# The last three tiles of a gated mixture kernel in an order written out by hand, on each engine

## The chip, the cores and the metric

The kernel runs on one core of a Trainium2 chip. The core has five engines with a queue each: TensorE (PE in the profile, with PEld for its weight loads), VectorE (DVE), ScalarE (ACT), GpSimd (POOL) and SyncE (SP). Each engine works through its own instructions in order; between engines, and between an instruction and an earlier result of its own engine, order is kept by semaphores. The metric is the device time of the core in microseconds, lower is better.

## The reference, cut to what matters

Rows `x` of 4 x 512 tokens with 512 numbers each go through two stages, both behind a layer norm and a gate:

```
x = x + tanh(g_xattn[0]) * xattn(layernorm(x), tokens, ctx, ctx, ctx)
x = x + tanh(g_ffn[0]) * ffn(layernorm(x), Wr, br, Wd, bd, Wu, bu)

def xattn(h, token_ids, Wg, Wu, Wd):     # 4 experts, picked by the token's number; here Wg = Wu = Wd
    y = (silu(h @ Wg[e].T) * (h @ Wu[e].T)) @ Wd[e]
def ffn(x, Wr, br, Wd, bd, Wu, bu):      # 8 experts of rank 16, the best two
    gates = softmax(x @ Wr + br + bonus)
    w = the two largest gates of a row, divided by their sum, else 0
    h = relu(x @ Wd[e] + bd[e])
    out = sum over e of w[e] * (h @ Wu[e] + bu[e])
```

## The kernel before

The rows are sorted by expert into T = 16 tiles of 128 rows. Since a tile can hold rows of several experts, NP = T + 3 = 19 pairs of a tile and an expert are worked through. For a pair, ACT normalizes the rows (`h`), PE turns them (`ps_hT`), and the expert's two products run (`ps_a`, then `ps_y`), each as three 16-bit products of high and low parts: ACT copies the high part out of PSUM, DVE subtracts it to get the low part. DVE adds the result to the rows (`add_y`, line 1082) and takes the sums for the second norm (`statistics2`, line 1090).

The second stage of a tile runs three steps (`LATE`) and more behind its pair: POOL gets the reciprocal root (`rstd`, line 454), ACT normalizes (`h2`, line 796), PE turns (`ps_h2T`, line 685), ACT and DVE make high and low parts (lines 815 and 1110), PE forms `ps_hid` (lines 632 to 634, "hidden product"), DVE adds the bias (`hid`, line 1124) and finds the two largest (`top8`, `gap`, `arg8`, lines 1142 to 1146). ACT takes the tanh of half the gap (line 801), POOL turns the indices into masks (`choice`, line 488), DVE blends them to the weights `w8`, the weighted rows (line 1172) and three copies of `w8` (`w_rep`, line 1176). PE turns these (`ps_wT`, lines 697 and 698), ACT and DVE make high and low parts again (lines 790 and 791; 1150 and 1151, "low parts of wtT"), PE forms the output product `ps_o` (lines 642 to 645), DVE adds it (`add_low_rank`, line 1113) and POOL scatters the tile to its rows in HBM (line 529).

Each engine's part of one step is the function `step`. `pipeline` (line 313) calls it for all steps: what a step does for each pair and tile it looks up by offsets, and equal steps go into a loop. The order in a step is thus written by hand once. The steps 19 to 22, in which no pair is begun, are drained by the same functions, with a few branches of their own (`ending` and `draining` on DVE, `has_y and not has_a` on PE). `choice` and `rstd` on POOL run in one loop over all steps (line 510). Tile numbers of a pair are read into registers (`place`, line 1077) before the add.

## Time and profile before

| | us |
|---|---|
| Median of 3 runs (lowest to highest) | 200.31 (199.83 to 200.53) |
| The profiled execution | 200.81 |
| Its span, from first to last instruction | 198.7 |
| PE busy | 173.7 (87%) |
| DVE busy | 155.5 (78%) |
| ACT busy | 105.9 (53%) |
| POOL busy | 99.5 (50%) |

A row of the profile gives an instruction by its line in the kernel, engine, operation and tiles (out<-in); times are counted from the start of the span. An instruction can begin before the one ahead of it on its engine has ended, so starts tell more of the order than busy time does. A name with a q at its end (DVEq) is the engine's sequencer, which handles registers and waits ahead of the engine itself. Tiles that end in a number lose it (`h2` stands as `h`, `w8` as `w`).

### The profile page before, as it was taken

What the parts mean: (1) busy time and instruction counts of PE and PEld (TensorE: products, weight loads), DVE (VectorE), ACT (ScalarE), POOL (GpSimd) and SP (SyncE); (2) the same over time, 40 slices, a digit from 0 to 9 for tenths busy, and PEclk for the clock granted to TensorE, in tenths of its full rate; (3) what the DMA queues carried; (4) which work ended last, traced back from release to release, by engine and by line L of the source; (5) the groups of instructions that cost most, each with busy time, mean ns of one, the idle gap of its engine ahead of it and who ended that gap; (6) DMA issues with size and microseconds to landing.
All of it is one profiled execution on the core that took longest, in us unless ns stands there. A gap on an engine that the chain in (4) does not pass through costs nothing.

```text
span 198.7 us, 4382 instructions
## 1 busy us (share of the span) xinstructions
PE 173.7 (87%) x1074; PEld 105.5 (53%) x1075; DVE 155.5 (78%) x523; ACT 105.9 (53%) x224; POOL 99.5 (50%) x246
## 2 busy tenths in 40 slices
PE   1666896999998999999999999999999999987550
PEld 1654473665554555756567565665655666553310
DVE  4859695797669799898988899877887778877840
ACT  3596599984576365363635646256462653415300
POOL 4477855508444475465735538336062351626551
PEclk9999999999999999999999999999999999999995
DMA  4937682000301201103011010110110101001121
GB/s 144 383 136 243 209 214 80 30 26 2 107 4 49 56 0 53 58 2 106 3 53 54 0 53 0 53 54 0 53 53 2 53 2 53 35 21 53 53 101 57
DMA packets 6784, 13.43 MB, mean 68 GB/s; under 512 B 2392, under 2 KB 2520, under 8 KB 6768
## 3 DMA queue, kind: packets, MB, share of 16 engines
q0 software_dynamic: 2560, 8.39, 12.6%
q1 hardware_dynamic: 4208, 4.86, 7.3%
q8 instruction: 6, 0.10, 0.2%
q14 instruction: 10, 0.08, 0.1%
HBM read 9.06 MB, written 4.19 MB: 67 GB/s over the span
## 4 chain that ended last, share of the span: by engine, by line
PE 66%; issue 7%; DMA 7%; DVE 7%; POOL 7%; SPq 1%; ACT 1%; POOLq 1%; DVEq 1%
PE ps_y L603 8%; PE ps_y L605 8%; PE ps_y L604 8%; PE ps_a L603 7%; PE ps_a L604 7%; PE ps_a L605 7%; PE ps_pT L624 4%; DMA xs<-in_x_dram,rows_of 4%; PE ps_h2T L685 3%; PE ps_hT L677 3%; DMA bu_nat<-in_L_ffn_bu_dram 3%; POOL hot_slot L432 2%; POOL xs L439 2%; PE ps_hid L632 2%; PE ps_hid L634 1%
## 5 line engine op out<-in xcount | busy, mean ns | idle before, releaser
L456 POOL TENSOR_SCALAR ve<-mv 128x1 f32<-128x1 f32 x32 | 7.6, 238 | 60.6 <-DVE mv L1099 50.1
L603 PE MATMUL ps_y<-w_hi,pT_hi 128*128 x76 | 28.8, 379 | 2.6 <-DVE w_lo L952 1.8
L783 ACT ACTIVATE pT_hi<-ps_pT 128x512 f16<-128x512 f32 x19 | 11.3, 595 | 36.0 <-PE ps_pT L624 36.0
L603 PE MATMUL ps_a<-w_hi,hT_hi 128*128 x76 | 29.6, 389 | 0.7 <-DVE hT_lo L1074 0.6
L604 PE MATMUL ps_a<-w_lo,hT_hi 128*128 x76 | 29.5, 388 | 0.0
L605 PE MATMUL ps_a<-w_hi,hT_lo 128*128 x76 | 29.3, 386 | 0.0
L604 PE MATMUL ps_y<-w_lo,pT_hi 128*128 x76 | 28.8, 379 | 0.0
L605 PE MATMUL ps_y<-w_hi,pT_lo 128*128 x76 | 28.8, 379 | 0.0
L796 ACT ACTIVATE h<-xs,mrs,rs 128x512 f32<-128x512 f32 (+1 forms) x16 | 13.0, 814 | 21.6 <-POOL mrs L458 21.6
L1086 DVE SCALAR_TENSOR_TENSOR xs<-ps_y,y_t,xs 128x512 f32 x19 | 14.3, 751 | 12.2 <-PE ps_y L605 11.5
L457 POOL TENSOR_TENSOR rs<-ve,neg_half 128x1 f32<-128x1 f32 x32 | 18.8, 587 | 2.7
L529 POOL DMA_INDIRECT out_dram<-xs,rows_of x16 | 17.3, 1082 | 5.0 <-DVE xs L1117 2.5
L824 ACT ACTIVATE h<-xs,mrs,rs 128x512 f32 (+1 forms) x19 | 15.6, 818 | 6.9 <-POOL mrs L458 4.3
L439 POOL DMA_INDIRECT xs<-in_x_dram,rows_of x16 | 17.0, 1063 | 3.7 <-issue 2.9
L805 ACT ACTIVATE silu<-ps_a,inv_bits 128x512 f32<-128x512 f32 x19 | 12.8, 675 | 4.3 <-PE ps_a L605 4.2
L1068 DVE SCALAR_TENSOR_TENSOR prod<-ps_a,prod_bits,silu 128x512 f32<-128x512 f32 x19 | 14.0, 739 | 1.1 <-ACT silu L805 1.1
L1104 DVE TENSOR_TENSOR pT_lo<-ps_pT,pT_hi 128x512 f16<-128x512 f32 x19 | 13.1, 689 | 0.7 <-ACT pT_hi L783 0.3
L1074 DVE TENSOR_TENSOR hT_lo<-ps_hT,hT_hi 128x512 f16<-128x512 f32 x19 | 12.9, 681 | 0.5 <-ACT hT_hi L810 0.3
L1117 DVE SCALAR_TENSOR_TENSOR xs<-ps_o,out_coef,xs 128x512 f32<-128x512 f32 (+1 forms) x16 | 11.9, 741 | 1.3 <-PE ps_o L645 1.2
L603 PEld LDWEIGHTS ps_y<-w_hi,pT_hi 128*128 128x128 f16 x76 | 7.6, 100 | 9.7 <-issue 3.0
L740 ACT ACTIVATE sq_act<-w_nat 128x512 f32<-128x512 f32 x16 | 10.1, 632 | 4.9 <-DMA w_nat<-in_ctx_dram 4.5
L605 PEld LDWEIGHTS ps_a<-w_hi,hT_lo 128*128 128x128 f16 x76 | 7.6, 100 | 9.2 <-issue 0.8
(209 smaller groups left out, 432.6 us busy)
## 6 DMA issues: line engine op xcount, KB each, us to landing
w_nat<-in_ctx_dram SPq DMA_DIRECT2D x4, 1024.0 KB, 7.5
xs<-in_x_dram,rows_of POOLq DMA_INDIRECT x16, 3.5
wd_nat<-in_L_ffn_Wd_dram SPq DMA_DIRECT2D x1, 256.0 KB
wu_nat<-in_L_ffn_Wu_dram SPq DMA_DIRECT2D x1, 256.0 KB
out_dram<-xs,rows_of POOLq DMA_INDIRECT x16, 2.9
b_in<-in_L_ffn_bd_dram SPq DMA_DIRECT2D x1, 64.0 KB
bu_nat<-in_L_ffn_bu_dram SPq DMA_DIRECT2D x3, 16.0 KB
tok_i<-in_itok_BxS_dram SPq DMA_DIRECT2D x1, 8.0 KB, 1.6
```

Source lines behind the costliest of these rows:

```text
L439: g.indirect_dma_start(out=xs[:, t, :], out_offset=None, in_=x_rows[:, :], in_offset=bass.IndirectOffsetOnAxis(ap=rows_of[:, t:t + 1], axi ...
L457: then(g.tensor_tensor(rs[:, n, k:k + 1], ve[:, n, k:k + 1], neg_half[:, :], ALU.pow))
L529: g.indirect_dma_start(out=out_rows[:, :], out_offset=bass.IndirectOffsetOnAxis(ap=rows_of[:, k:k + 1], axis=0), in_=x1[:, k, :], in_offse ...
L603: mm(ps[:, :], lhs_hi[:, kc, :], hi, start=(kc == 0), stop=False)
L604: mm(ps[:, :], lhs_hi[:, kc, :], lo, start=False, stop=False)
L605: last = mm(ps[:, :], lhs_lo[:, kc, :], hi, start=False, stop=(kc == KC - 1))
L796: a(h2[:, :], flat(x1[:, col(k), :]), ACT.Identity, bias=mrs[:, 1, col(k)], scale=rs[:, 1, col(k)]).then_inc(normed2, 1)
L824: a(h[:, :], flat(xs[:, col(tile), :]), ACT.Identity, bias=mrs[:, 0, col(tile)], scale=rs[:, 0, col(tile)]).then_inc(normed1, 1)
L1068: v.scalar_tensor_tensor(prod[:, :], ps_a[:, :], prod_t[:, col(k)], silu[:, :], ALU.mult, ALU.mult).then_inc(prod_done, 1)
L1074: v.tensor_tensor(hT_lo[:, :, :], ps_hT[:, :, :], hT_hi[:, :, :], ALU.subtract).then_inc(hT_lo_done, 1)
L1086: v.scalar_tensor_tensor(flat(x1[:, col(tile), :]), ps_y[:, :], y_t[:, col(k)], flat(xs[:, col(source), :]), ALU.mult, ALU.add).then_inc(x ...
L1104: v.tensor_tensor(pT_lo[:, :, :], ps_pT[:, :, :], pT_hi[:, :, :], ALU.subtract).then_inc(pT_lo_done, 1)
```

## The change

All steps up to 18 stay as they are; `pipeline` stops there. For the rest every engine gets a function `drain` that lists its instructions one by one for the tiles 12 to 15.

- The second norm of tiles 14 and 15: DVE adds the epsilon (`variance`), POOL takes the power only, and DVE normalizes (`norm2`), where POOL did three instructions and ACT the normalization.
- The masks of tiles 13 to 15: DVE makes them (`choose`) instead of POOL.
- The copies of `w8` for tiles 13 to 15 are made by ACT (`repeat_w`) instead of DVE.
- The output product of tiles 12 and 13 is taken out of PSUM by ACT (`take_out`) and added by POOL (`add_taken`) instead of by DVE.
- Tile 15 is turned into two PSUM banks (`ps_hT`, `ps_pT`), two quarters in each, and its high and low parts are made by halves.
- The order of the rest is new. On PE the hidden product of tile 13 stands ahead of the transposes of the last expert product.

```diff
+                if first == NP:
+                    break
+                last = min(last, NP)
...
+            def scatter(k, done=None):
+
+                pool.wait_ge(*(done or (out_done, k + 1)))
+                g.indirect_dma_start(
+                    out=out_rows[:, :],
+                    out_offset=bass.IndirectOffsetOnAxis(ap=rows_of[:, k:k + 1], axis=0),
+                    in_=x1[:, k, :], in_offset=None,
+                ).then_inc(s_scatter, 16)
+
+            def power(n, k):
+
+                pool.wait_ge(var_done, n)
+                g.tensor_tensor(rs[:, 1, k:k + 1], ve[:, 1, k:k + 1], neg_half[:, :],
+                                ALU.pow).then_inc(rstd2, 1)
+
+            def add_taken(n, k):
+
+                pool.wait_ge(o_taken, n)
+                g.tensor_tensor(x1[:, k, :], taken[:, n - 1, :], x1[:, k, :],
+                                ALU.add).then_inc(added, 1)
+
+            for i in range(-3, NP):
...
-                if 0 <= k < T:
+                if 0 <= k < T - 2:
                     pool.wait_ge(aggr2, k + 1)
                     rstd(1, mv2, k, rstd2)
+
+            scatter(T - 5)
+            power(1, T - 2)
+            power(2, T - 1)
+            add_taken(1, T - 4)
+            scatter(T - 4, (added, 1))
+            add_taken(2, T - 3)
+            scatter(T - 3, (added, 2))
+            scatter(T - 2, (out_done, T - 3))
+            scatter(T - 1, (out_done, T - 2))
...
+            def drain():
+
+                last = NP - 1
+                e_last = expert_of(last)
+                hidden_product(T - 3)
+                transpose_product(last)
+                second_product(last, e_last)
+                transpose_h2(T - 2)
+                low_rank_out(T - 4)
+                hidden_product(T - 2)
+
+                pe.wait_ge(normed2, T)
+                for c in range(KC):
+                    half = tr((ps_hT, ps_pT)[c // 2][:, c % 2, :], h2[:, c:D:KC], ident[:, :])
+                    if c % 2:
+                        half.then_inc(h2T_last, 1)
+                pe.wait_ge(w_rep_done, 1)
+                transpose_weighted(T - 3)
+
+                pe.wait_ge(hid_done, T - 1)
+                for c in range(KC):
+                    pe.wait_ge(lo_last, c // 2 + 1)
+                    mm(ps_hid[:, 0:HC], hT_hi[:, c, :], w_in_hi[:, c, :], start=(c == 0), stop=False)
+                    mm(ps_hid[:, 0:HC], hT_hi[:, c, :], w_in_lo[:, c, :], start=False, stop=False)
+                    done = mm(ps_hid[:, 0:HC], hT_lo[:, c, :], w_in_hi[:, c, :],
+                              start=False, stop=(c == KC - 1))
+                done.then_inc(hid_mm, 1)
+                low_rank_out(T - 3, (o_taken, 1))
+                pe.wait_ge(w_rep_done, 2)
+                transpose_weighted(T - 2)
+                low_rank_out(T - 2, (o_taken, 2))
+                pe.wait_ge(w_rep_done, 3)
+                transpose_weighted(T - 1)
+                low_rank_out(T - 1, (out_done, T - 3))
+
...
+            def repeat_w(n, k):
+
+                act.wait_ge(w8_done, k + 1)
+                act.wait_ge(wtT_done, k)
+                a(w_rep[:, :, 0:EF], w8[:, :].unsqueeze(1).to_broadcast([P, 3, EF]), ACT.Copy,
+                  scale=s_ffn[:, 0:1]).then_inc(w_rep_done, 1)
+
+            def take_out(n, k):
+
+                act.wait_ge(o_mm, k + 1)
+                a(taken[:, n - 1, :], ps_o[:, :], ACT.Copy, scale=out_coef[:, :]).then_inc(o_taken, 1)
+
+            def drain():
+
+                pT_high(NP - 1)
+                wtT_high(T - 4)
+                tanh_of_gap(T - 3)
+                h2T_high(T - 2)
+                take_out(1, T - 4)
+                repeat_w(1, T - 3)
+                for n, bank in enumerate((ps_hT, ps_pT)):
+                    act.wait_ge(h2T_last, n + 1)
+                    a(hT_hi[:, 2 * n:2 * n + 2, :], bank[:, 0:2, :], ACT.Copy).then_inc(hi_last, 1)
+                wtT_high(T - 3)
+                tanh_of_gap(T - 2)
+                repeat_w(2, T - 2)
+                take_out(2, T - 3)
+                wtT_high(T - 2)
+                tanh_of_gap(T - 1)
+                repeat_w(3, T - 1)
+                wtT_high(T - 1)
+
...
+            def variance(n, k):
+
+                dve.wait_ge(aggr2, k + 1)
+                v.tensor_scalar(ve[:, 1, k:k + 1], mv2[:, 1:2], EPS, None, ALU.add).then_inc(var_done, 1)
+
+            def norm2(k):
+
+                dve.wait_ge(rstd2, k + 1)
+                dve.wait_ge(h2T_done, k)
+                v.tensor_scalar(h2[:, :], x1[:, k, :], mv2[:, 0:1], rs[:, 1, k:k + 1],
+                                ALU.subtract, ALU.mult).then_inc(normed2, 1)
+
+            mixed = [0]
+
+            def then_mix(ins):
+
+                mixed[0] += 1
+                ins.then_inc(mix_step, 1)
+                dve.wait_ge(mix_step, mixed[0])
+
+            def choose(n, k):
+
+                dve.wait_ge(arg_done, k + 1)
+                then_mix(v.tensor_copy(arg8f[:, :], arg8[:, :]))
+                v.tensor_scalar(half_first[:, :], slot_no[:, 0:EF], arg8f[:, 0:1], 0.5,
+                                ALU.is_equal, ALU.mult)
+                then_mix(v.tensor_scalar(half_second[:, :], slot_no[:, 0:EF], arg8f[:, 1:2], 0.5,
+                                         ALU.is_equal, ALU.mult))
+                v.tensor_tensor(half_sum[:, :], half_first[:, :], half_second[:, :], ALU.add)
+                v.tensor_tensor(half_dif[:, :], half_first[:, :], half_second[:, :],
+                                ALU.subtract).then_inc(mixed_last, 1)
+                dve.wait_ge(mixed_last, n)
+                dve.wait_ge(tanh_done, k + 1)
+
+            def drain():
+
+                pT_low(NP - 1)
+                statistics2(T - 2)
+                variance(1, T - 2)
+                hidden(T - 3)
+                top_two(T - 3)
+                choose(1, T - 3)
+                wtT_low(T - 4)
+                norm2(T - 2)
+                add_y(NP - 1, *place(NP - 1))
+                statistics2(T - 1)
+                variance(2, T - 1)
+                h2T_low(T - 2)
+                norm2(T - 1)
+                dve.wait_ge(wtT_done, T - 3)
+                blend(T - 3).then_inc(weighted_done, 1)
+                hidden(T - 2)
+                top_two(T - 2)
+                for n, bank in enumerate((ps_hT, ps_pT)):
+                    dve.wait_ge(hi_last, n + 1)
+                    v.tensor_tensor(hT_lo[:, 2 * n:2 * n + 2, :], bank[:, 0:2, :],
+                                    hT_hi[:, 2 * n:2 * n + 2, :], ALU.subtract).then_inc(lo_last, 1)
+                wtT_low(T - 3)
+                choose(2, T - 2)
+                dve.wait_ge(wtT_done, T - 2)
+                dve.wait_ge(w_rep_done, 1)
+                blend(T - 2).then_inc(weighted_done, 1)
+                hidden(T - 1)
+                top_two(T - 1)
+                wtT_low(T - 2)
+                choose(3, T - 1)
+                dve.wait_ge(wtT_done, T - 1)
+                dve.wait_ge(w_rep_done, 2)
+                blend(T - 1).then_inc(weighted_done, 1)
+                add_low_rank(T - 2)
+                wtT_low(T - 1)
+                add_low_rank(T - 1)
```

PE around the end of step 18, before (hidden product of tile 13: `ps_hid`; transposes of the last product: `ps_pT`):

```order
L697 MATMUL ps_wT<-ident,weighted 128x128 [waits wtT_lo_done,weighted_done]
L698 MATMUL ps_wT<-ident,w_rep 96x128
L610 TENSOR_LOAD expert_i
L610 ISA x2
L624 MATMUL ps_pT<-ident,prod 128x128 [waits prod_done]
L624 MATMUL ps_pT<-ident,prod 128x128 x3
L632 MATMUL ps_hid<-w_in_hi,h2T_hi 128x136 [waits hid_done,h2T_lo_done]
L633 MATMUL ps_hid<-w_in_lo,h2T_hi 128x136
L634 MATMUL ps_hid<-w_in_hi,h2T_lo 128x136
```

and now:

```order
L700 MATMUL ps_wT<-ident,weighted 128x128 [waits wtT_lo_done,weighted_done]
L701 MATMUL ps_wT<-ident,w_rep 96x128
L649 TENSOR_LOAD expert_i
L649 ISA x2
L671 MATMUL ps_hid<-w_in_hi,h2T_hi 128x136 [waits hid_done,h2T_lo_done]
L672 MATMUL ps_hid<-w_in_lo,h2T_hi 128x136
L673 MATMUL ps_hid<-w_in_hi,h2T_lo 128x136
...
L673 MATMUL ps_hid<-w_in_hi,h2T_lo 128x136
L663 MATMUL ps_pT<-ident,prod 128x128 [waits prod_done]
L663 MATMUL ps_pT<-ident,prod 128x128 x3
L642 ISA [waits x1_done,pT_lo_done]
L642 MATMUL ps_y<-w_hi,pT_hi 128x512
```

The 12 matmuls of the hidden product now stand ahead of the four transposes, and with these all that waits for `pT_lo_done`.

DVE from the search for the indices of tile 13 to the registers of the last add of `ps_y`, before:

```order
L1146 MAX_INDEX arg8<-top8,hid 128x8
L1150 TENSOR_TENSOR wtT_lo<-ps_wT,wtT_hi 128x128 [waits wtT_hi_done]
L1151 TENSOR_TENSOR gwT<-ps_wT,gwT 8x128
L1079 TENSOR_LOAD pair_tile_i
L1079 ISA x2
L1080 TENSOR_LOAD source_i
L1080 ISA x2
L1086 ISA [waits x1_done,y_done]
L1086 REGISTER_ALU
L1086 SCALAR_TENSOR_TENSOR xs<-ps_y,y_t,xs 128x512
```

and now:

```order
L1255 MAX_INDEX arg8<-top8,hid 128x8
L1336 CAST arg8f<-arg8 128x8 [waits arg_done]
L1337 TENSOR_SCALAR half_first<-slot_no,arg8f 128x8 [waits mix_step]
L1339 TENSOR_SCALAR half_second<-slot_no,arg8f 128x8
L1341 TENSOR_TENSOR half_sum<-half_first,half_second 128x8 [waits mix_step]
L1342 TENSOR_TENSOR half_dif<-half_first,half_second 128x8
L1260 TENSOR_TENSOR wtT_lo<-ps_wT,wtT_hi 128x128 [waits wtT_hi_done,tanh_done,mixed_last]
L1261 TENSOR_TENSOR gwT<-ps_wT,gwT 8x128
L1322 TENSOR_SCALAR h2<-xs,mv2,rs 128x512 [waits h2T_done,rstd2]
L1200 TENSOR_LOAD pair_tile_i
L1200 ISA x2
L1201 TENSOR_LOAD source_i
```

Five instructions of the masks have come in between, and the low parts of wtT (`wtT_lo`, first row of two) wait for the last of them (`mixed_last`) and for the tanh; the normalization of tile 14 (`h2`) follows, and the register loads come behind them.

POOL in the drain, before (scatter of tile 11, norm of tile 15, first instruction of the choice of tile 14):

```order
L529 DMA out_0_dram<-xs,rows_of 2048x512 [waits out_done]
L456 TENSOR_SCALAR ve<-mv2 128x1 [waits aggr2]
L457 TENSOR_TENSOR rs<-ve,neg_half 128x1 [waits rs_step]
L458 TENSOR_SCALAR mrs<-mv2,rs 128x1 [waits rs_step]
L491 CAST arg8f<-arg8 128x8 [waits arg_done]
```

and now, from the scatter of tiles 10 and 11 to the last:

```order
L526 DMA out_0_dram<-xs,rows_of 2048x512 [waits out_done] x2
L535 TENSOR_TENSOR rs<-ve,neg_half 128x1 [waits var_done] x2
L541 TENSOR_TENSOR xs<-taken,xs 128x512 [waits o_taken]
L526 DMA out_0_dram<-xs,rows_of 2048x512 [waits added]
L541 TENSOR_TENSOR xs<-taken,xs 128x512 [waits o_taken]
L526 DMA out_0_dram<-xs,rows_of 2048x512 [waits added]
L526 DMA out_0_dram<-xs,rows_of 2048x512 [waits out_done] x2
```

The power of tile 15 (the second of the two `rs`) is followed at once by the add of tile 12, which waits for ACT's copy alone.

## Rows read from the trace of the kernel before

**Rows 1.** Stretches: us, busy of each engine (instructions), granted clock, DMA share, GB/s.
```profile
175.00:185.00 10.00, 7.34 (x52) 4.19 (x50) 7.93 (x32) 4.29 (x11) 4.75 (x14) 1.00 0.07 28
185.00:195.00 10.00, 4.85 (x28) 2.01 (x28) 6.01 (x20) 1.33 (x6) 5.78 (x13) 0.90 0.20 79
```

**Rows 2.** PE in order of time: start us, us, line, operation, out<-in.
```profile
175.02 0.22 PE L632 MATMUL ps_hid<-w_in_hi,h2T_hi 128*128 128x136 f16 x1
...
175.67 0.22 PE L634 MATMUL ps_hid<-w_in_hi,h2T_lo 128*128 128x136 f16 x1
```

**Rows 3.** DVE in order of time from 175 us.
```profile
175.85 0.69 DVE L1104 TENSOR_TENSOR pT_lo<-ps_pT,pT_hi 128x512 f16<-128x512 f32 x1 [0.29 <-ACT pT_hi L783]
...
177.20 0.18 DVE L1099 BATCH_NORM_AGGREGATE mv<-st 128x2 f32<-128x6 f32 x1
...
177.29 0.28 DVE L1124 TENSOR_TENSOR hid<-ps_hid,b_s 128x136 f32<-128x136 f32 x1
...
178.00 0.15 DVE L1146 FIND_INDEX8 arg<-top,hid 128x8 uint32<-128x8 f32 x1
...
179.71 0.75 DVE L1086 SCALAR_TENSOR_TENSOR xs<-ps_y,y_t,xs 128x512 f32 x1 [1.08 <-PE ps_y L605]
...
181.24 0.18 DVE L1099 BATCH_NORM_AGGREGATE mv<-st 128x2 f32<-128x6 f32 x1
```

**Rows 4.** DVE's sequencer, 176 to 181 us: durations ns, first to last start.
```profile
L1079 DVEq TENSOR_LOAD <-pair_tile_i x1: 304/304/304, 177.8 to 177.8; - x1
...
L1080 DVEq SEQ_ASSERT  x1: 23/23/23, 179.0 to 179.0; - x1
...
L1086 DVEq FUSED_REGOPS  x1: 105/105/105, 179.5 to 179.5; - x1
```

**Rows 5.** DVE in order of time at 22 us, each waiting for the one before.
```profile
22.30 0.15 DVE L987 CAST half_exp_f<-half_exp 128x2 f32<-128x2 int32 x1
22.48 0.36 DVE L989 TENSOR_SCALAR exp_of<-expert_f,half_exp_f 128x2 f32<-128x2 f32 x2
22.87 0.16 DVE L992 TENSOR_REDUCE exp_t<-exp_of 128x2 f32<-128x4 f32 x1
```

**Rows 6.** POOL in order of time: variance and power of tile 15.
```profile
181.52 0.24 POOL L456 TENSOR_SCALAR ve<-mv 128x1 f32<-128x1 f32 x1 [0.16 <-DVE mv L1099]
181.84 0.57 POOL L457 TENSOR_TENSOR rs<-ve,neg_half 128x1 f32<-128x1 f32 x1
```

**Rows 7.** The last tile in order of time, ACT and DVE.
```profile
182.92 0.81 ACT L796 ACTIVATE h<-xs,mrs,rs 128x512 f32<-128x512 f32 x1
...
185.19 0.69 DVE L1110 TENSOR_TENSOR h2T_lo<-ps_h2T,h2T_hi 128x512 f16<-128x512 f32 x1 [0.23 <-ACT h2T_hi L815]
...
187.08 0.74 DVE L1117 SCALAR_TENSOR_TENSOR xs<-ps_o,out_coef,xs 128x512 f32<-128x512 f32 x1
...
187.75 0.16 DVE L1142 MAX8 top<-hid 128x8 f32<-128x8 f32 x1
...
190.07 0.29 DVE L1172 SCALAR_TENSOR_TENSOR weighted<-hid,w 128x128 f32<-128x128 f32 x1
...
191.51 0.29 DVE L1150 TENSOR_TENSOR wtT_lo<-ps_wT,wtT_hi 128x128 f16<-128x128 f32 x1 [0.22 <-ACT gwT L791]
...
193.34 0.75 DVE L1117 SCALAR_TENSOR_TENSOR xs<-ps_o,out_coef,xs 128x512 f32<-128x512 f32 x1 [1.24 <-PE ps_o L645]
```

**Rows 8.** Groups by line and shape: count, busy us, mean ns, idle before.
```profile
L506 POOL TENSOR_TENSOR w_lo<-w_full,w_hi 128x512 f16<-128x512 f32 x2 | 2.3, 1155 | 7.4 <-ACT w_hi L752 7.4
...
L1029 DVE TENSOR_SCALAR b_s<-b_in,ffn_bits 128x136 f32<-128x136 f32 x1 | 0.3, 258 | 0.0
```

**Rows 9.** POOL beside DVE at 7.7 us, in order of time.
```profile
7.71 1.77 POOL L432 TENSOR_SCALAR hot_slot<-slot_no,in_tile_f 128x128 f16<-128x128 f32 x1 [4.68 <-DVE in_tile_f L916]
...
7.86 1.22 DVE L919 TENSOR_TENSOR hot_slot<-in_tile_f,slot_no 128x1024 f16<-128x1024 f16 x1
```

**Rows 10.** POOL's line 432: count, ns min/median/max, first and last start.
```profile
L432 POOL TENSOR_SCALAR hot_slot<-slot_no,in_tile_f x4: 600/788/1767, 7.7 to 11.0; 128x128 f16<-128x128 f32 x4
```

174 lines of the change are left out of this document (86 added, 88 removed).

## The prediction

> **What bounds the kernel now.** I read the page first, then busy time by stretches, then instructions in order of time over the last 25 us, since the change touches nothing before that. On the page PE is busy 87% of a span of 198.7 us, and its tenths stand at 9 until slice 35, from about 174 us on at 8, 7, 5, 5, 0. The reader is to see in the stretches [rows 1] that DVE outlasts PE there: from 175 to 185 us it is busy 7.93 of 10 us beside PE's 7.34, from 185 to 195 us 6.01 beside 4.85. So the drain (the steps after the last pair has begun) hangs on a chain that runs through DVE again and again, and what an engine idles matters less than when DVE comes to an instruction. The granted clock is 1.00 to 185 us and 0.90 after it; the page's last slice has it at half, its lower level.
>
> Everything below is a walk along DVE's instructions, step against step, with tile 15 (the last) as the one that ends the kernel. The difference in the time at which its last add starts is the forecast, because what follows that add (one scatter, its transfer, the end) is the same in both kernels.
>
> **Step 1, PE: hidden product before the transposes.** Before, PE turns the last product first and then runs the hidden product of tile 13; the change swaps them. The hidden product is 12 matmuls; the first starts at 175.02 and the twelfth at 175.67 [rows 2], 0.059 each, 0.71 in all. The transposes, ACT's copy, DVE's subtraction (start 175.85 [rows 3]) and the last expert product each come 0.71 later. Nothing hides it: DVE waits for the subtraction, and the hidden product was lying in that wait before.
>
> **Step 2, DVE: variance and choice of tile 13.** The variance waits for the aggregate's result. Before, the next instruction (hid, 177.29) was issued 0.09 after the aggregate (177.20) [rows 3]; now the aggregate's 0.18, 0.03 for the wait and some 0.08 to issue lie between: +0.20. So the index search, 178.00 before [rows 3], stands at 178.91. Then come the five instructions of the choice, which POOL did beside. Their waits are priced from three DVE instructions early in the kernel that wait for each other just so [rows 5]: a cast to the next instruction 0.18, a pair of masks to the next 0.39. With 0.19 from the search to the cast and 0.28 for sum and difference (an estimate: 0.16 and 0.03 as in those rows, and the other instruction's issue) that is 1.04: release at 179.95. The bounds: 0.65, if half the waits go under; 1.35, with POOL's slower durations.
>
> **Step 3, DVE: the registers of the last y-add.** Before, DVE's sequencer ran ahead: the first register load stands at 177.8, before the search at 178.00 had even started, and the last check at 179.0 [rows 4]; 1.22 us, hidden behind the expert product. In the change the instruction in front of those loads that waits is the low part of wtT, which waits for the choice's last result. So they begin at 179.98 and end at 181.20. From the operation on registers at 179.5 [rows 4] to the add at 179.71 [rows 3] is 0.2; with the release 0.25. The add starts at 181.45, against 179.71: +1.74. The expert product (0.71 late) is ready well before. The low parts of wtT for tile 12 and the normalization of tile 14 run under these loads and cost nothing; if the loads could still run ahead (0.6 instead of 1.22, the lower bound), they'd be what stands there, and 0.6 comes back.
>
> **Step 4, the norm of tile 15.** From add to aggregate start is 1.53 [rows 3], its length 0.18; variance 0.19; handing to POOL 0.10 (181.42 to 181.52), the power 0.57 [rows 6], and 0.09 back: the normalization starts at 184.11. Before, ACT's started at 182.92 [rows 7], so +1.19: a gain of 0.55 within the step. ACT took 0.81 for it [rows 7]. No row has DVE's 128x512 scalar operation from SBUF; the same operation with 136 elements takes 0.258 [rows 8], with 2 elements 0.22 (0.36 for two, of which the second starts 0.14 later [rows 5]), so 0.36 at 512 by that slope; upper bound 0.74, the 128x512 add with a scalar (187.08 [rows 7]). I take 0.36, the row of the same operation: end at 184.47 against 183.73, +0.74. At 0.74 the whole would come 0.4 later.
>
> **Step 5, turning tile 15 into two banks.** PE is free for it at 184.72, and ACT's two half copies are ready at about 185.5 and 185.8 (0.38 each, an estimate from the page's 0.595 for the whole). DVE gets there no sooner: normalization, blend of tile 13, hid and search of tile 14 hold it to 185.78 (0.29, 0.6 and 0.78, the last from 177.29 to 178.00 [rows 3] and one issue). Two half subtractions end at 186.51; before, the whole one ended at 185.88 [rows 7]: +0.63. The halves bring nothing that DVE could use.
>
> **Step 6, the queue after it.** DVE now does the low parts of wtT for tile 13 (0.59: two instructions of 0.29 [rows 7]), choice and blend of tile 14 (0.9 and 0.6), and only then hid of tile 15, at 188.5, although PE has had it since 187.1. The maximum follows at 188.84. Before it stood at 187.75, held there by the add of 187.08 [rows 7], which is now taken over by ACT and POOL: +1.09 (without that help +1.7). Low parts of tile 14, wait for ACT's copy, choice of tile 15: its weighted rows start at 191.23, against 190.07: +1.16. The repeat of w8 on ACT lies beside weighted and saves 0.15; the half clock that stretched the last matmuls before (0.1) is already in the row. Last add at 194.2 against 193.34 [rows 7]: **+0.86**.
>
> POOL's two adds of 128x512 take some 1.15 each (its subtraction of that shape, [rows 8]) and end, scatters included, by 191.5, before the scatter of tile 14 can go: nothing on the path. ACT's two copies of the output product: idle time of ACT, 5.6 of the 20 us busy.
>
> Against its own profiled execution (200.81, span 198.7 and 2.1 around it) the sum gives 201.7. That execution lay 0.5 above the median of the runs, 200.31; on the median the sum gives **201.2**. A measurement of this kernel tells about 0.3% (0.6 us) from no change.
>
> **A wait of DVE on POOL (rival B).** In this trace a POOL instruction that reads SBUF beside a DVE instruction with two SBUF inputs is the one that waits: POOL's mask at 7.71 took 1.77 while DVE's 1.22 ran from 7.86 [rows 9], where its shortest took 0.60 [rows 10]; DVE's 1024 elements kept their 1.2. In the change, POOL's first add starts the moment its power for tile 15 ends (184.02), 0.09 before DVE's normalization of tile 15, and lasts 1.15. If DVE waits for it, the normalization starts at 185.15 and every later step moves by 1.0: +1.9, 202.2. For it: the add comes first, and nothing of DVE in this trace is of this kind and size. Against it: in rows 9 DVE wasn't held.
>
> The Trainium skill, SBUF — State Buffer, section "Who interferes with whom", states that DVE's scalar operation from SBUF to SBUF can take both port pairs, and that then whichever of DVE and POOL starts first has the shared pair for its whole instruction. By that rule the normalization is held, as in rival B; the trace agrees for POOL's side alone (1.77 in place of 0.60), and no run here shows DVE's.
>
> **Rival C, the clock.** PE will idle more between 175.3 and 177.4 and after 180 us. The clock fell once before, in the last 6 us. If it falls by 185 us, the hidden products (0.71 each), the turns and the output products run at the lower level; on the path that is some 0.3 for tile 15's hidden product and 0.75 for its output product (3 times 0.21 more): +1.6 to +2, 202.1. For it: more idle; against it: with PE busy only 4.85 of 10 us the clock still stood at 0.90 over 185 to 195 us [rows 1].
>
> **Rival D, faster: DVE's queue doesn't bind.** Then only tile 15's own chain counts: norm by POOL 0.55 shorter, normalization 0.45, half copies 0.5, the add of 187.08 no longer ahead of the maximum 0.65, choice 0.6, w8 0.15: -2.9, and +0.9 for steps 1 and 2: -2.0, 198.3; with half of it 199.3. It decides from the point where the last y-add starts within 0.3 of the expert product, 180.4 instead of 181.45. For it: each of these gains is real on its own. Against it: DVE was busy 79% of 175 to 185 us already [rows 1], and the change adds three choices (some 2.7), two normalizations (0.6) and two variances (0.4) and removes two adds (1.3) and three repeats (0.5).
>
> **Rival E, no change:** loads still ahead (-0.6) and choices at their lower bound; 200.3.
>
> **How the numbers follow.** Forecast (0.5 to 1.4 more) 0.45; B 0.20; C 0.08; D 0.17; E 0.10. Forecast, B and C lie over +0.6 with 0.31, 0.19, 0.08: slower 0.58. Within 0.6: 0.14, 0.09 from E and 0.02 of D: 0.25. Faster: 0.17 (0.15 of D, 0.02 of the others). The range reaches from the middle of D and E, 199.6, to B and C, 202.4; the forecast's own is 200.8 to 201.7.
>
> **What would show it.** Right: the last y-add 1.5 us or more after the end of DVE's last choice mask, DVE hardly idle from 184 to 192 us, the last maximum some 2 us after its PE product. B: the last normalization takes 1.4 or begins after POOL's add ends. Wrong: y-add within 0.3 of the expert product, the transposes not 0.7 later, or a choice under 0.6.

## The result and the profile after

The changed kernel takes 203.95 us (median of 4 runs, 203.21 to 205.87), against 200.07 for the kernel before on the same chip: ratio 1.0213, 95% interval [1.0128, 1.0299]. The forecast was 201.2, its range ended at 202.4. Slower was right; the size was not. The profiled execution took 203.24, its span is 201.5. Now and then one execution of a kernel takes 1.5% or more above the fastest of that kernel; such ones are left out of all medians and ratios here.

First the stretches of the changed kernel, in the columns of [rows 1]:

```profile
175.00:185.00 10.00, 6.02 (x42) 3.26 (x39) 7.98 (x29) 2.50 (x6) 2.55 (x4) 1.00 0.08 28
185.00:195.00 10.00, 5.80 (x31) 3.55 (x32) 8.55 (x38) 3.96 (x14) 4.17 (x5) 0.83 0.14 53
```

VectorE (DVE) has as much to do as before in the first ten microseconds and 2.5 us more in the second ten (8.55 against 6.01), although two of its adds went to other engines. To set the steps against those of before, both traces need a common point: the y-add of pair 17, the last instruction ahead of the drain. In the trace before, and then in the changed kernel's with the instructions that answer to [rows 3] and [rows 7]:

```profile
174.81 0.75 DVE L1086 SCALAR_TENSOR_TENSOR xs<-ps_y,y_t,xs 128x512 f32 x1 [0.48 <-PE ps_y L605]
```

```profile
174.66 0.75 DVE L1207 SCALAR_TENSOR_TENSOR xs<-ps_y,y_t,xs 128x512 f32 x1 [0.48 <-PE ps_y L644]
...
176.43 0.69 DVE L1225 TENSOR_TENSOR pT_lo<-ps_pT,pT_hi 128x512 f16<-128x512 f32 x1 [1.01 <-ACT pT_hi L848]
...
178.76 0.16 DVE L1255 FIND_INDEX8 arg<-top,hid 128x8 uint32<-128x8 f32 x1
178.95 0.17 DVE L1336 CAST arg8f<-arg 128x8 f32<-128x8 uint32 x1
...
179.84 0.29 DVE L1260 TENSOR_TENSOR wtT_lo<-ps_wT,wtT_hi 128x128 f16<-128x128 f32 x1
...
180.46 0.55 DVE L1322 TENSOR_SCALAR h<-xs,mv,rs 128x512 f32<-128x512 f32 x1
181.49 0.75 DVE L1207 SCALAR_TENSOR_TENSOR xs<-ps_y,y_t,xs 128x512 f32 x1 [0.48 <-issue]
...
184.04 1.48 DVE L1322 TENSOR_SCALAR h<-xs,mv,rs 128x512 f32<-128x512 f32 x1
...
186.91 0.40 DVE L1368 TENSOR_TENSOR hT_lo<-ps_hT,hT_hi 128x256 f16<-128x256 f32 x1
...
190.15 0.17 DVE L1251 MAX8 top<-hid 128x8 f32<-128x8 f32 x1
...
190.95 0.29 DVE L1260 TENSOR_TENSOR wtT_lo<-ps_wT,wtT_hi 128x128 f16<-128x128 f32 x1 [0.30 <-ACT gwT L855]
...
191.57 0.40 DVE L1336 CAST arg8f<-arg 128x8 f32<-128x8 uint32 x1
...
193.00 0.29 DVE L1269 SCALAR_TENSOR_TENSOR weighted<-hid,w 128x128 f32<-128x128 f32 x1
...
196.16 0.75 DVE L1238 SCALAR_TENSOR_TENSOR xs<-ps_o,out_coef,xs 128x512 f32<-128x512 f32 x1 [1.27 <-PE ps_o L687]
```

Ahead of the last y-add (181.49), VectorE's sequencer (DVEq) loads its two registers (durations in ns, first to last start):

```profile
L1200 DVEq TENSOR_LOAD <-pair_tile_i x1: 314/314/314, 179.9 to 179.9; - x1
...
L1201 DVEq SEQ_ASSERT  x1: 23/23/23, 181.1 to 181.1; - x1
```

The line to look at is 184.04: the same instruction that took 0.55 for tile 14 (180.46) takes 1.48 for tile 15. The cast, 0.17 for tile 13, takes 0.40 for tile 15 (191.57). Neither row shows a wait before its start: the instruction begins and then lasts longer. GpSimd (POOL) in the same trace, its power and its two adds:

```profile
183.45 0.55 POOL L535 TENSOR_TENSOR rs<-ve,neg_half 128x1 f32<-128x1 f32 x1 [4.66 <-DVE ve L1316]
183.97 1.27 POOL L541 TENSOR_TENSOR xs<-taken,xs 128x512 f32<-128x512 f32 x1
...
190.69 1.25 POOL L541 TENSOR_TENSOR xs<-taken,xs 128x512 f32<-128x512 f32 x1 [4.13 <-ACT taken L878]
```

The normalization lies beside the first add (183.97 to 185.24), the cast beside the second (190.69 to 191.94), and they end 0.28 and 0.03 us after it. ScalarE (ACT) ahead of the low parts of tile 14 (190.95):

```profile
189.91 0.69 ACT L878 ACTIVATE taken<-ps_o,out_coef 128x512 f32<-128x512 f32 x1 [0.19 <-PE ps_o L687]
190.49 0.27 ACT L854 ACTIVATE wtT_hi<-ps_wT 128x128 f16<-128x128 f32 x1
```

Last, TensorE (PE) and its clock: the stretches of five microseconds, and two successive hidden products of tile 15.

```profile
185.00:190.00 5.00, 4.09 (x24) 3.00 (x24) 4.50 (x21) 2.11 (x8) 1.27 (x2) 0.66 0.14 52
190.00:195.00 5.00, 1.71 (x9) 0.54 (x8) 4.05 (x18) 1.85 (x7) 2.89 (x3) 1.00 0.14 54
```

```profile
187.53 0.32 PE L727 MATMUL ps_hid<-w_in_lo,hT_hi 128*128 128x136 f16 x1
187.64 0.32 PE L728 MATMUL ps_hid<-w_in_hi,hT_lo 128*128 128x136 f16 x1
```

They start 0.11 apart where those of [rows 2] stood 0.06 apart: the granted clock was at its lower level (1.2 GHz) there, 0.66 as a mean over 185 to 190 us, and back at 1.00 after it.

### The profile page after: what moved, and what is told of

Read it like the earlier page. It is cut to its first block, busy times and chain, and to the rows that moved or that the text cites. A ratio compares the mean times of both kernels' runs of the same rounds, so it can differ in the third digit from the quotient of the medians.

```text
span 201.5 us, 4385 instructions
## 1 busy us (share of the span) xinstructions
PE 172.6 (86%) x1074; PEld 105.3 (52%) x1075; DVE 159.1 (79%) x538; ACT 106.4 (53%) x228; POOL 97.1 (48%) x229
## 4 chain that ended last, share of the span: by engine, by line
PE 65%; DVE 10%; DMA 7%; issue 6%; POOL 5%; SPq 1%; DVEq 1%; ACT 1%; POOLq 1%
PE ps_y L642 7%; PE ps_y L644 7%; PE ps_y L643 7%; PE ps_a L642 7%; PE ps_a L643 6%; PE ps_a L644 6%; DMA xs<-in_x_dram,rows_of 4%; PE ps_pT L663 4%; PE ps_h2T L693 3%; PE ps_hT L767 3%; DMA bu_nat<-in_L_ffn_bu_dram 2%; POOL hot_slot L445 2%; PE ps_hid L671 2%; POOL xs L452 2%; PE ps_hid L673 2%
## 5 line engine op out<-in xcount | busy, mean ns | idle before, releaser
L469 POOL TENSOR_SCALAR ve<-mv 128x1 f32<-128x1 f32 x30 | 7.1, 238 | 56.5 <-DVE mv L1220 45.2
L642 PE MATMUL ps_a<-w_hi,hT_hi 128*128 x76 | 28.8, 379 | 0.7 <-DVE hT_lo L1195 0.6
L643 PE MATMUL ps_a<-w_lo,hT_hi 128*128 x76 | 28.8, 379 | 0.0
L644 PE MATMUL ps_a<-w_hi,hT_lo 128*128 x76 | 28.8, 379 | 0.0
L921 ACT ACTIVATE h<-xs,mrs,rs 128x512 f32<-128x512 f32 (+1 forms) x14 | 11.4, 815 | 18.9 <-POOL mrs L471 18.9
L470 POOL TENSOR_TENSOR rs<-ve,neg_half 128x1 f32<-128x1 f32 x30 | 17.7, 588 | 2.5
L671 PE MATMUL ps_hid<-w_in_hi,h2T_hi 128*128 128x136 f16 x60 | 11.3, 223 | 1.6 <-DVE h2T_lo L1231 1.6
L767 PE MATMUL ps_hT<-ident,h 128*128 128x128 f32 x76 | 12.0, 281 | 0.6 <-ACT h L944 0.6
```

Source lines behind the costliest of these rows:

```text
L470: then(g.tensor_tensor(rs[:, n, k:k + 1], ve[:, n, k:k + 1], neg_half[:, :], ALU.pow))
L642: mm(ps[:, :], lhs_hi[:, kc, :], hi, start=(kc == 0), stop=False)
L643: mm(ps[:, :], lhs_hi[:, kc, :], lo, start=False, stop=False)
L644: last = mm(ps[:, :], lhs_lo[:, kc, :], hi, start=False, stop=(kc == KC - 1))
L671: mm(ps_hid[:, 0:HC], h2T_hi[:, c, :], w_in_hi[:, c, :], start=(c == 0), stop=False)
L767: last = tr(ps_hT[:, c, :], h[:, c * P:(c + 1) * P], ident[:, :])
```

## The experiments

Fourteen kernels ran, in four sets, on the chips numbered 7 (a0, e1, e4, e5), 3 (c1 to c4), 11 (d1 to d4) and 15 (g1, g2), each with the kernel before beside it. The medians of the kernel before there are 201.26, 201.05, 201.06 and 201.01, so between sets compare the column "over", the median less the kernel before's of the same set. The last three columns come from each one's profiled execution, in microseconds after the y-add of pair 17: the last y-add, the weighted rows of tile 15, the last add.

| Kernel | median us (runs) | over | ratio to before [95%] | last y-add | weighted 15 | last add |
|---|---|---|---|---|---|---|
| before, first chip | 200.07 (4) | | | 4.90 | 15.26 | 18.53 |
| changed, first chip | 203.95 (4) | 3.88 | 1.0213 [1.0128, 1.0299] | 6.83 | 18.34 | 21.50 |
| a0: changed again | 203.56 (6) | 2.30 | 1.0154 [1.0093, 1.0214] | 6.82 | 18.65 | 21.68 |
| e1: first add later | 203.59 (5) | 2.33 | 1.0100 [1.0066, 1.0133] | 6.81 | 19.18 | 23.32 |
| e4: e1, loads, turn first | 202.90 (7) | 1.64 | 1.0092 [1.0060, 1.0124] | 5.87 | 17.03 | 21.17 |
| e5: 16 idle products | 203.79 (7) | 2.53 | 1.0129 [1.0098, 1.0160] | 6.82 | 17.94 | 21.82 |
| c1: both adds clear | 202.50 (11) | 1.45 | 1.0072 [1.0046, 1.0099] | 6.82 | 16.77 | 20.91 |
| c2: adds on VectorE | 203.89 (5) | 2.84 | 1.0137 [1.0103, 1.0172] | 6.82 | 18.33 | 22.21 |
| d4: c1, loads | 201.59 (8) | 0.53 | 1.0031 [1.0004, 1.0058] | 6.36 | 16.29 | 20.17 |
| c3: c1, loads, turn first | 201.15 (12) | 0.10 | 1.0003 [0.9980, 1.0027] | 5.87 | 15.82 | 19.95 |
| c4: c2, loads, turn first | 202.71 (6) | 1.66 | 1.0099 [1.0060, 1.0137] | 5.86 | 17.32 | 21.20 |
| d1: c3, idle products at the end | 200.69 (12) | -0.37 | 1.0000 [0.9970, 1.0029] | 5.86 | 15.85 | 18.88 |
| d2: c3, choice of 13 on GpSimd | 200.27 (12) | -0.79 | 0.9963 [0.9941, 0.9985] | 5.12 | 15.08 | 19.21 |
| d3: d1 and d2 | 199.76 (11) | -1.30 | 0.9956 [0.9923, 0.9989] | 5.12 | 15.07 | 18.11 |
| g1: changed, 28 idle products | 202.79 (11) | 1.78 | 1.0061 [1.0024, 1.0099] | 6.82 | 17.96 | 20.99 |
| g2: c1, 13 idle products | 201.74 (11) | 0.73 | 1.0041 [1.0006, 1.0076] | 6.82 | 17.54 | 20.57 |

**a0, the changed kernel again.** No edit.

> The changed kernel once more, beside the three edits of it that follow. Both theories: some 3 to 4 us over the kernel before, with DVE's normalization of tile 15 at about 1.5 us and a lower clock somewhere between 185 and 190 us. Open is why its runs spread from 203.2 to 205.9 while those of before lay within 1.3 us.

Measured 203.56, 2.30 over the kernel before, less than the 3 to 4 expected; normalization 1.48, cast 0.40 as on the first chip. Both holds thus came in both traces.

**e1, the first add later.** GpSimd's first add waits until VectorE's normalization of tile 15 has ended:

```diff
+            pool.wait_ge(normed2, T)
             add_taken(1, T - 4)
```

> POOL's first add waits until the normalization of tile 15 has ended. Theory hold (POOL's add of 128x512, begun 0.07 us earlier, holds DVE's normalization for its whole length): the normalization takes 0.55 instead of 1.48 us and the last add starts about 0.9 us earlier, so the time falls by 0.7 to 1.2 us. Rival clock (the excess over the forecast is TensorE's lower clock from 185 to 189 us): the normalization may shorten, but the time falls by less than 0.3 us.

The normalization went back to 0.55, and yet the median stayed, 2.33 over the kernel before, as the rival had it. (The ratio fell, from 1.0154 to 1.0100, but the intervals overlap. The profiled execution took 205.41, so of it only durations are read.) VectorE and then GpSimd in e1:

```profile
184.34 0.55 DVE L1323 TENSOR_SCALAR h<-xs,mv,rs 128x512 f32<-128x512 f32 x1
184.80 0.22 DVE L1267 SCALAR_TENSOR_TENSOR w<-half_dif,half_tanh,half_sum 128x8 f32<-128x8 f32 x1
185.06 1.33 DVE L1270 SCALAR_TENSOR_TENSOR weighted<-hid,w 128x128 f32<-128x128 f32 x1
```

```profile
184.97 1.27 POOL L541 TENSOR_TENSOR xs<-taken,xs 128x512 f32<-128x512 f32 x1 [0.66 <-DVE h L1323]
```

The add now lay beside the weighted rows, whose two inputs both come from SBUF: 1.33 in place of 0.29. The hold had not gone, it had moved by two instructions. So the kind of instruction counts that lies beside the add, not this one place. In this trace the granted clock was 0.67 over 185 to 190 us and 0.50 over 190 to 195 as well.

**e4, e1 with loads early and the transposes first.** The row address of the last y-add is loaded at the start of the drain, and PE turns the last product before the hidden product of tile 13:

```diff
+                where_last = place(NP - 1)
                 pT_low(NP - 1)
...
-                add_y(NP - 1, *place(NP - 1))
+                add_y(NP - 1, *where_last)
...
+                transpose_product(last)
                 hidden_product(T - 3)
-                transpose_product(last)
```

> Three edits at once: POOL's add waits as in the run before, DVE loads the registers of the last y-add at the start of the drain, PE turns the last product ahead of the hidden product of tile 13. Theory queue and hold: the last y-add starts about 1.3 us earlier than in the changed kernel (0.7 by the turn, 0.6 by the loads), the last add 2.2 us earlier (with 0.9 from the hold): 201 to 201.5 us where the changed kernel takes 203.3. Rival clock: all three move DVE but the end moves by less than 0.8 us, since PE's slow stretch stays.

The last y-add came 0.96 earlier, at 5.87; the weighted rows of tile 13 were held again (1.33), the clock stood at its lower level for the last output product, and 202.90 came out instead of 201 to 201.5: a miss.

**e5, idle products.** Sixteen products of 128x512 into a bank that nobody reads any more, in PE's pauses from the transposes of the last pair to those of tile 15 (`idle_products(n)` repeats one matmul n times).

> The changed kernel with 16 more products of 128x512 on PE, whose results nobody reads, laid where PE idled between 175.5 and 185.5 us (6 before the last expert product, 3 behind it, 5 and 2 around the hidden product of tile 14). Theory hold: the clock stays at 1.00 from 185 to 190 us and the last add starts 0.4 to 0.9 us earlier, no more; the normalization still takes 1.5. Rival clock: the time falls by 2 us or more and the spread of the runs falls to that of before.

The clock, then, in three stretches of e5:

```profile
185.00:190.00 5.00, 3.60 (x34) 2.27 (x33) 4.67 (x17) 1.86 (x7) 2.81 (x3) 1.00 0.13 52
190.00:195.00 5.00, 2.69 (x17) 0.98 (x14) 4.36 (x24) 1.77 (x6) 2.24 (x2) 1.00 0.01 2
195.00:199.00 4.00, 2.29 (x6) 0.58 (x6) 1.77 (x4) 0.44 (x2) 0.96 (x1) 0.66 0.34 131
```

It stayed at 1.00 where the changed kernel had 0.66, and the weighted rows of tile 15 came at 17.94 instead of 18.34. It then fell at the last output product, whose matmuls took 0.61 to 0.63, and the gain was lost; neither theory had this. The time alone would have said that the clock doesn't matter. (This execution took 205.60, and 2 us of that lie ahead of the drain: its y-add of pair 17 stands at 176.66, in the other traces at 174.1 to 175.3.)

**c1, both adds clear.** Both adds are kept, but each starts where VectorE reads PSUM and one SBUF tile:

```diff
+            pool.wait_ge(arg_done, T - 1)
             add_taken(1, T - 4)
             scatter(T - 4, (added, 1))
+            pool.wait_ge(weighted_done, T)
             add_taken(2, T - 3)
```

> The changed kernel, but GpSimd's two adds start at places where VectorE reads PSUM and one SBUF tile: the first after the index search of tile 14 (it then lies beside the half subtractions and the low parts of wtT), the second after the weighted rows of tile 15. Theory 1 (GpSimd's 128x512 add, both inputs from SBUF, holds VectorE's instructions that need both SBUF read ports, wherever it starts): the normalization of tile 15 takes 0.55 instead of 1.48, the weighted rows of tile 13 0.29 (they took 1.33 in e1), the cast of tile 15 0.17 instead of 0.40; the last add, 21.5 us after the add of pair 17 in the changed kernel, comes at 20.3 to 20.6, time 202.3 to 202.6. Rival (what counts is TensorE's lower clock or the length of VectorE's queue, and the holds are taken up by other waits, as e1 seemed to say): the three durations shrink, but the last add stays after 21.2 and the time over 203.2.

VectorE and GpSimd in c1:

```profile
184.12 0.55 DVE L1324 TENSOR_SCALAR h<-xs,mv,rs 128x512 f32<-128x512 f32 x1
...
184.83 0.29 DVE L1271 SCALAR_TENSOR_TENSOR weighted<-hid,w 128x128 f32<-128x128 f32 x1
...
186.32 0.41 DVE L1370 TENSOR_TENSOR hT_lo<-ps_pT,hT_hi 128x256 f16<-128x256 f32 x1
186.65 0.28 DVE L1262 TENSOR_TENSOR wtT_lo<-ps_wT,wtT_hi 128x128 f16<-128x128 f32 x1
...
190.36 0.17 DVE L1338 CAST arg8f<-arg 128x8 f32<-128x8 uint32 x1
```

```profile
186.16 1.26 POOL L541 TENSOR_TENSOR xs<-taken,xs 128x512 f32<-128x512 f32 x1 [2.08 <-DVE arg L1257]
...
191.90 1.25 POOL L541 TENSOR_TENSOR xs<-taken,xs 128x512 f32<-128x512 f32 x1 [3.13 <-DVE weighted L1271]
```

All three held instructions have their own length back, and the two that now lie beside the first add (186.32 and 186.65, one input from PSUM) keep theirs: 0.41 and 0.28, against 0.41 and 0.29 in the changed kernel, where no add lies beside them. The weighted rows of tile 15 come at 16.77 instead of 18.65 in a0, and the time over the kernel before is 1.45 instead of 2.30. From the weighted rows to the last add it takes 4.14, in a0 3.03: the last output product of c1 ran at the lower clock.

```profile
193.72 0.61 PE L686 MATMUL ps_o<-wu_hi,wtT_hi 128*128 128x512 f16 x1 [1.15 <-DVE gwT L1263]
194.12 0.63 PE L687 MATMUL ps_o<-wu_lo,wtT_hi 128*128 128x512 f16 x1
```

The theory had the durations and the time (202.50) right, the last add a little too early (20.91 for 20.3 to 20.6), because of that clock.

**c2 and c4, the adds back on VectorE.** VectorE adds tile 12 where it waits for GpSimd's power, tile 13 ahead of the low parts of wtT(14); ACT's copies and GpSimd's adds are gone. c4 has the loads and the order of e4 as well.

```diff
                 h2T_low(T - 2)
+                add_low_rank(T - 4)
                 norm2(T - 1)
...
                 top_two(T - 1)
+                add_low_rank(T - 3)
                 wtT_low(T - 2)
...
```

> The changed kernel, but VectorE adds tiles 12 and 13 itself, out of PSUM: tile 12 between the low part of h2T(14) and the normalization of tile 15, where it waits for GpSimd's power anyway, tile 13 before the low parts of wtT(14). ACT's two copies and GpSimd's two adds are gone. Theory 1: no VectorE instruction is held (0.55, 0.29, 0.17 us); the first add costs 0.1 to 0.2 beyond the wait it fills, the second about 0.4; the last add at 20.7 to 21.0 after the add of pair 17, 202.7 to 203.0. Rival (taking two adds from VectorE was worth their 0.66 each, as the change intends): the last add comes at 21.9 or later, 203.9 or more.

> c2_dve_adds with the loads early and the transposes first. Theory: last y-add at 5.87, last add at 19.8 to 20.0, 201.8 to 202.0. Rival: 202.7 or more.

A miss: no hold is left, but 203.89 and 202.71, each over 1 us above its twin with the adds on GpSimd (c1 202.50, c3 201.15). The clock fell earlier than in the twin (0.90, 0.76 and 0.93 over the three stretches from 180 to 195 us in c2, 1.00, 1.00 and 0.63 in c1); no run separates its share from that of the adds. The rival's times (203.9 and 202.7 or more) came: with nothing held, the two adds on VectorE cost more than a microsecond, the clock's share included.

**d4 and c3, the steps 1 and 3 of the prediction undone.** d4 is c1 with the loads early, c3 also has PE's old order (both edits as in e4).

> c1_clear with the register loads of the last y-add at the start of the drain, and no other change: half of what lies between c1 and c3. Theory (loads, then the choice and the normalization queued before the add, decide): y-add at 6.25 to 6.4 instead of 6.82, last add at 20.3 to 20.5 instead of 20.91, time 202.0 to 202.2; the other 0.5 to 0.9 to c3 then is the order of product and transposes. Rival (the loads alone made the whole delay of step 3): y-add at 5.7, time 201.4.

> c1_clear with the register loads of the last y-add at the start of the drain and the last product turned before the hidden product of tile 13. Theory: the three parts add: last y-add at 5.87 as in e4 (6.83 in the changed kernel, 4.90 before), last add at 19.4 to 19.6, 201.4 to 201.6. Rival (some other chain, TensorE at its lower clock, takes over): last add at 20.5, 202.5, as little as e4 gained.

The y-adds came as the theories had them (6.36 and 5.87), the times a little lower than expected, c3's last add later (19.95 for 19.4 to 19.6). Over the kernel before, the loads bring 0.92 (1.45 to 0.53), the order of product and transposes another 0.43 (to 0.10); the last add moves by 0.74 and 0.22. c3 takes as long as the kernel before.

**d1, d2, d3, on from there.** d1 is c3 with 13 idle products around the turns of the last two tiles' weighted rows; d2 is c3 with the choice of tile 13 left on GpSimd, between its two powers; d3 is both.

```diff
             power(1, T - 2)
+            choice(T - 3)
             power(2, T - 1)
...
                 top_two(T - 3)
-                choose(1, T - 3)
                 wtT_low(T - 4)
...
```

> c3_clear_three with 13 idle 128x512 products on TensorE in its pauses between 187.4 and 193 us (2 and 5 around the turn of the weighted rows of tile 14, 2 and 4 around that of tile 15), each 0.22 long, into a bank that nobody reads any more. Theory (the lower clock at the end costs the four last output matmuls 0.2 each and the turn 0.15): those matmuls take 0.38 to 0.39 instead of 0.61 to 0.63, the last add comes 0.8 to 1.0 earlier (19.0 to 19.2 after the add of pair 17, from 19.95), time 200.2 to 200.5. Rival (the fall of the clock is only put off to the next piece, as in e5, or comes earlier): no gain, 201.1.

> c3_clear_three with the choice of tile 13 on GpSimd, between its two powers, as the kernel before has it. Theory (VectorE's queue decides in front of the last y-add): the y-add comes at 5.0 to 5.2 instead of 5.87, the last add at 19.1 to 19.3 instead of 19.95, time 200.3 to 200.5. Rival (GpSimd's small masks and VectorE's instructions with two SBUF inputs hold each other, or the power of tile 15 comes late): y-add at 5.1 but the blend of tile 13 late, last add after 19.7, 201.0.

> d1 and d2 together: if each does what its theory says, last add at 18.2 to 18.5, time 199.4 to 199.8, below the kernel before; else what remains of the two.

In d1 the last output product ran at the full clock, with the stretch at 1.00 where c3 had 0.61 (the stretch in c3 and in d1, then d1's output product):

```profile
190.00:195.00 5.00, 3.26 (x10) 0.79 (x7) 2.38 (x10) 0.75 (x3) 3.21 (x3) 0.61 0.13 52
190.00:195.00 5.00, 2.88 (x13) 0.94 (x11) 2.54 (x6) 0.75 (x3) 3.52 (x4) 1.00 0.15 58
```

```profile
192.16 0.39 PE L686 MATMUL ps_o<-wu_hi,wtT_hi 128*128 128x512 f16 x1 [0.29 <-DVE gwT L1272]
192.39 0.38 PE L687 MATMUL ps_o<-wu_lo,wtT_hi 128*128 128x512 f16 x1
```

The last add is 1.07 earlier than in c3's trace, the time 0.47 lower, and the ratios (1.0003 and 1.0000) don't tell the two apart. c3's profiled execution was its longest (202.00), so its clock may have cost less in the others; that is not shown. In d2 the choice on GpSimd brings the last y-add to 5.12, where it waits for the expert product again, and 0.89 of the time:

```profile
179.19 0.75 DVE L1210 SCALAR_TENSOR_TENSOR xs<-ps_y,y_t,xs 128x512 f32 x1 [0.31 <-PE ps_y L647]
```

d2 and d3 are faster than both kernels; d3 takes 199.76, ratio 0.9956 [0.9923, 0.9989], within the 199.4 to 199.8 expected.

**g1 and g2, the clock's share.** g1 is the changed kernel, holds and all, with idle products through the whole drain; g2 is c1 with 13 of them at the end, so neither holds nor, as meant, the lower clock.

> The changed kernel, holds and all, with 28 idle 128x512 products in TensorE's pauses from the last pair's transposes to the last output product (the 16 of e5 and 12 more around the turns of the weighted rows of tiles 14 and 15). Theory (of the time over the forecast, the holds of VectorE by GpSimd's adds and TensorE's lower clock are two separate parts): normalization of tile 15 still 1.4 to 1.5, cast of tile 15 still held, but every output matmul at 0.38 to 0.39; weighted rows of tile 15 at 17.9 to 18.0 as in e5, last add at 20.8 to 20.95 (21.5 to 21.7 in the changed kernel), time 202.9 to 203.1. Rival (the clock was of no consequence): last add after 21.4, 203.5.

> c1_clear with 13 idle products around the turns of the weighted rows of tiles 14 and 15: the changed kernel with neither the holds nor the lower clock, and so the case that the forecast of the prediction walked through. If the walk was right but for these two, weighted rows of tile 15 at 16.7 to 16.8 after the add of pair 17 (the walk: 16.42), last add at 19.9 to 20.05 (the walk: 19.39), time 201.9 to 202.2. Rival (a third part is missing): weighted rows or last add 0.5 later than that.

In g1 the clock stood at 1.00 throughout, while the normalization still took 1.48 and the cast 0.34:

```profile
185.00:190.00 5.00, 3.39 (x27) 1.94 (x25) 4.50 (x21) 2.02 (x8) 1.40 (x2) 1.00 0.13 52
190.00:195.00 5.00, 4.60 (x22) 1.82 (x22) 4.04 (x18) 1.67 (x7) 3.14 (x3) 1.00 0.14 54
```

Last add 20.99, time 202.79: the clock's own share in the changed kernel is 0.52 of the time (2.30 in a0 to 1.78), 0.5 to 0.7 in the traces. g2 has 201.74, ratio 1.0041. Its profile was less clean than meant, since the clock fell ahead of the idle products there:

```profile
180.00:185.00 5.00, 2.63 (x18) 1.89 (x19) 4.25 (x13) 1.58 (x3) 0.55 (x1) 0.85 0.02 3
185.00:190.00 5.00, 4.68 (x33) 3.03 (x32) 3.95 (x20) 2.33 (x9) 2.30 (x2) 0.81 0.08 30
```

```profile
185.56 0.30 DVE L1256 TENSOR_TENSOR hid<-ps_hid,b_s 128x136 f32<-128x136 f32 x1 [0.56 <-PE ps_hid L675]
```

VectorE waited 0.56 for the hidden product of tile 14 there. That put its weighted rows at 17.54, against 16.7 to 16.8 expected, and the last add at 20.57; from the one to the other it is 3.03, as at the full clock in d1. c1, with the same program up to the output product of tile 13, had its weighted rows at 16.77, with the clock at 1.00 to 190 us.

## Why the prediction was wrong

The step that failed is the overlap of GpSimd's two adds with VectorE. The prediction's sum has "nothing on the path" for them; the runs show that each held a VectorE instruction that was on it, the normalization of tile 15 for 0.93 us and the cast of tile 15 for 0.23. Beside that the normalization was mis-sized (0.36 for 0.55), and the fall of the clock, which the sum leaves out, came.

Step by step, in microseconds after the y-add of pair 17 (174.81 taken from the walk's times), with c1 as the same program without these two holds:

| | walk | changed | c1 |
|---|---|---|---|
| step 1: pT_lo starts | 1.75 | 1.77 | 1.76 |
| step 2: choice releases | 5.14 | 5.18 | 5.17 |
| step 3: last y-add | 6.64 | 6.83 | 6.82 |
| step 4: normalization of tile 15 starts | 9.30 | 9.38 | 9.38 |
| step 4: it ends | 9.66 | 10.86 | 9.93 |
| step 6: last MAX8 | 14.03 | 15.49 | 14.42 |
| step 6: weighted rows of tile 15 | 16.42 | 18.34 | 16.77 |
| last add | 19.39 | 21.50 | 20.91 |

**Steps 1 to 3** hold to 0.2 us: the swap on PE, the choice (1.04 by the walk, 1.08 from the search at 178.76 to the low part at 179.84), and register loads that can't run ahead. They stand at 179.9 to 181.1, and in the changed row of the y-add what ends its idle time is "issue", no longer PE: the sequencer is late, not the data. The edits of d4 and c3 gave both back: the y-add comes 0.46 and 0.49 earlier, where the forecast had 0.6 and 0.71 (the 0.49 lacks 0.22 that the early loads cost, see below).

**Step 4** went wrong in two ways. The length of an unhindered normalization is 0.55, not 0.36: it lies between the bounds of 0.36 and 0.74, and the end that was taken, from a row of 136 elements, was the wrong one (+0.19). And the hold by GpSimd's add, put aside as rival B with a chance of 0.20, did come: 1.48 for 0.55, +0.93, where B's sign was 1.4. c1 takes it away by a place for the add alone.

**Step 5** came out in its sense: in the changed kernel the first half subtraction starts (186.91) right behind the index search of tile 14, so VectorE was what the halves waited for.

**Step 6** had the queue right: MAX8 of tile 15 came 1.74 after the end of its product in c1, as in the walk (188.84 less 187.1). It missed the second hold. The prediction checked the one instruction that the first add meets, and said of GpSimd's adds that nothing of them lies on the path. The second add lies beside the choice of tile 15, which the change itself had put on VectorE: cast +0.23. ACT's copy of tile 13, "idle time of ACT" in the prediction, stood on the path too, since its output product came late (rival C below): the high parts of tile 14 start behind it (189.91, then 190.49), and VectorE's low parts wait 0.30 for them (190.95). With both holds gone, MAX8 and the weighted rows of c1 stand 0.39 and 0.35 behind the walk, most of which is there by the end of the normalization (0.27). From the weighted rows to the last add the walk takes 2.97, against 3.27 before, and gives a reason for 0.15 of these 0.30, or 0.25 with the half clock's 0.1; at the full clock it took 3.03 (g1, d1), so the end was about right without its sum being complete.

**Rival C**, the clock, was half true as well. It was to fall by 185 us and cost 0.3 at tile 15's hidden product and 0.75 at its output product. It fell in 185 to 190 us, over the turns and the hidden product of tile 15 and the first matmul of the next output product, and again only at the last matmul of all (0.51 for 0.38). The first fall made the output product of tile 13 late, and with it ACT's copy and VectorE's low parts of tile 14. Together it cost 0.52 by the times of a0 and g1. The reason given against it (4.85 busy of 10 us and still 0.90 before) did not carry over: with 5.80 busy the clock was 0.83.

In the changed kernel's trace the last add stands 2.11 behind the walk: 1.16 are the two holds, 0.19 the length of the normalization, 0.30 the wait for ACT, 0.13 the last matmul; 0.33 are small lags that no run separates.

So the forecast described the case without B and C, and that case is g2: ratio 1.0041 [1.0006, 1.0076], where +0.86 on 200.31 is 1.0043. The agreement is in part luck. The interval is wide, the trace was not free of the clock, and the forecast took the 2.1 us around the span to be the same in both kernels. On the chips of the experiments they are 2.09 to 2.20 in every run of the kernel before and 1.70 to 1.88 in every run of the others, so some 0.4 is gained outside the span, for a reason that no run shows; the span of g2 is 1.1 longer than before (200.0 against 198.9). What the changed kernel takes beyond g2 is the holds, 0.85 (a0 to c1) or 1.05 (g1 to g2), and the clock, 0.52 (a0 to g1) or 0.72 (c1 to g2). These shares are estimates: the intervals of the four ratios overlap, all but a0's with g2's, and the durations in the traces are the firmer evidence. (On the chips of the experiments the change costs 2.30; on the first it was 3.88, from four runs of 203.21 to 205.87 us, of which only that of 203.24 has a trace, so the other 1.6 stay open.) The two rivals were given apart, each as if the other failed; the range ended where one of them came true, and both did.

What misled was one reading of [rows 9]. There GpSimd's instruction, started 0.15 earlier, was the one that grew, and it was taken to speak against a hold of VectorE. It showed that such a pair can hold one another; which one loses it did not show for the pairs to come. Here GpSimd started 0.07 (184.04) and 0.09 us (e1) ahead and VectorE lost for as long as the add lasted.

The Trainium skill, SBUF — State Buffer, section "Who interferes with whom", names just these instructions: a scalar operation or a cast in a two-port mode, and any VectorE instruction with two SBUF inputs beside a GpSimd instruction that reads SBUF. It adds that one with at most one SBUF input and outside such a mode does not contend. The runs agree on each: 1.48 for 0.55, 0.40 for 0.17, 1.33 for 0.29, and 0.41 and 0.28 unchanged beside c1's add; in which mode an instruction ran no trace shows. That whichever starts first has the pair, as the prediction cites it, the starts in the traces bear out for GpSimd's adds, but not in [rows 9], where GpSimd started first and lost.

In c3 the first low part starts 0.22 later (1.26) than before (1.04), although PE's order is alike. The chain of c3's profile shows why: the early register loads stand in front of it and end only then.

```profile
176.16 0.02 DVEq L1203
176.19 0.05 issue
176.23 0.70 DVE pT_lo L1227
```

The same 0.22 is all that is left of the y-add's delay in d2 (5.12 against 4.90). Loads behind the low part were not tried.

Not settled: why the clock falls at a different place from one execution to the next of nearly the same program (180 to 190 us in g2, after 190 in c1), and why the changed kernel's runs spread as they do (203.10 to 205.97 in a0). No run was made for either.
